# Feed-forward opening of a decoder layer: the LayerNorm chain of three tiles moved one step ahead, the first ten gate and up products put into two banks in turn, tile 0's butterflies moved between engines

## What is computed

```python
gate = bitlinear(x, w_gate)          # x: (4, 512, 512), w_gate, w_up: (2048, 512)
up = bitlinear(x, w_up)
intermediate = jax.nn.silu(gate) * up
return h_bitlinear(intermediate, w_down)     # w_down: (512, 2048)
...
def bitlinear(x, w):   return jnp.einsum('bsh,oh->bso', act_quant(x), weight_quant(w))
def h_bitlinear(x, w): return jnp.einsum('bsh,oh->bso', act_quant(fwht(x)), weight_quant(w))
```

## Time and profile before

| | us |
|---|---|
| median of 3 runs | 1610.19 |
| lowest and highest | 1608.81, 1610.94 |
| time of the profiled execution | 1610.17 |
| its span, first to last instruction | 1608.3 |
| PE busy in the span | 1542.3 (96%) |
| POOL busy | 1268.9 (79%) |
| DVE busy | 1235.6 (77%) |
| ACT busy | 1175.4 (73%) |
| feed-forward block in the span | from 1300.5 to the end |

### The profile page before, as it was taken

How to read it: one execution, slowest core, us unless ns; L and a number is a source line. 1 busy time by engine, 2 the same in 40 slices (tenths; PEclk the granted TensorE clock), 3 DMA queues, 4 the chain that set the end, 5 groups by cost and what they waited for, 6 DMA issues and landing times. The chain is left out here.

```text
span 1608.3 us, 23916 instructions
## 1 busy us (share of the span) xinstructions
PE 1542.3 (96%) x7487; PEld 1069.7 (67%) x7520; DVE 1235.6 (77%) x2254; ACT 1175.4 (73%) x1950; POOL 1268.9 (79%) x1141
## 2 busy tenths in 40 slices
PE   8989999999999998999999999999999978999997
PEld 4577787787788756666666666766656535666665
DVE  2499989878877756787977888778888676776776
ACT  2454556788755435999999899989998937887873
POOL 0487787787787724899999999999999949988870
PEclk9999999999999998999999999999999999999999
DMA  7324251433312005111312032101201230010000
GB/s 249 118 71 92 81 94 47 114 117 120 118 40 94 33 29 167 41 46 29 109 38 63 21 104 67 32 22 43 77 9 48 122 125 1 28 40 27 21 21 27
DMA packets 57190, 110.24 MB, mean 69 GB/s; under 512 B 9244, under 2 KB 13596, under 8 KB 56682
## 3 DMA queue, kind: packets, MB, share of 16 engines
q1 hardware_dynamic: 55488, 107.64, 22.4%
q10 hardware_dynamic: 1578, 1.07, 0.2%
HBM read 71.26 MB, written 18.88 MB: 56 GB/s over the span
## 5 line engine op out<-in xcount | busy, mean ns | idle before, releaser
L1443 POOL TENSOR_TENSOR x_p_lo<-x_p,x_p_hi 128x1024 fp32r<-128x1024 f32 x255 | 603.3, 2393 | 59.0 <-ACT x_p_hi L1209 34.5
L1345 DVE TENSOR_REDUCE x_maxes<-x_ps_a 128x1 f32<-128x1024 f32 x252 | 306.8, 1217 | 114.5 <-PE x_ps_a L1544 110.9
L1172 ACT ACTIVATE x_p<-x_ps_b,x_any_valid 128x1024 f32<-128x1024 f32 x256 | 285.0, 1113 | 55.5 <-PE x_ps_b L1524 49.6
L1209 ACT ACTIVATE x_p_hi<-x_p 128x1024 fp32r<-128x1024 f32 x256 | 271.2, 1059 | 6.3
L1524 PE MATMUL x_ps_b<-x_Q,x_K 103*128 103x512 f32 x512 | 218.9, 509 | 12.1 <-ACT x_p L1172 10.1
L1584 PE MATMUL x_ps_o<-x_p_hi,x_V 128*96 128x512 f32 x512 | 208.4, 407 | 2.8 <-POOL x_p_lo L1443 2.2
L1585 PE MATMUL x_ps_o<-x_p_lo,x_V 128*96 128x512 f32 x512 | 201.4, 393 | 0.0
L1544 PE MATMUL x_ps_a<-x_K,x_Q 99*128 99x512 f32 x504 | 164.5, 407 | 4.7 <-POOL x_Q L1431 2.8
L1524 PEld LDWEIGHTS x_ps_b<-x_Q,x_K 103*128 103x128 f32 x512 | 87.6, 191 | 106.2 <-issue 58.3
L447 ACT ACTIVATE a_aT_hi<-a_ps_a 128x512 fp32r<-128x512 f32 x64 | 38.3, 598 | 150.5 <-PE a_ps_a L732 124.1
L458 ACT ACTIVATE a_work<-a_ps_s,a_neg_max,a_q_r 128x128 f32<-128x128 f32 x256 | 114.1, 465 | 9.9 <-DVE a_neg_max L553 9.8
(11 more groups left out here) (297 smaller groups left out, 3992.0 us busy)
## 6 DMA issues: line engine op xcount, KB each, us to landing
shared<-in_L_ffn_w_gate SPq DMA_DIRECT2D x16, 512.0 KB, 4.0
shared<-in_L_ffn_w_up SPq DMA_DIRECT2D x16, 512.0 KB, 4.2
shared<-in_L_ffn_w_down SPq DMA_DIRECT2D x16, 512.0 KB, 4.2
shared<-in_ctx SPq DMA_DIRECT2D x8, 1024.0 KB, 7.4
x_scratch<-rows SPq DMA_DIRECT2D x31, 256.0 KB, 2.0
x_Q<-x_q_hi SPq DMA_DIRECT2D x112, 64.0 KB, 2.0
shared<-in_L_attn_out_w SPq DMA_DIRECT2D x6, 1024.0 KB, 8.3
ffn_quant<-shared SPq DMA_DIRECT2D x24, 256.0 KB, 4.5
```

Source lines behind the costliest of these rows:

```text
L1172: act.activation(p[:, v % 3, :, :], ps_b[:, :, :], ACT.Exp, scale=any_valid[:, b % 2:b % 2 + 1]).then_inc(exp_ready, 1)
L1209: act.activation(p_hi[:, r], p[:, v % 3], ACT.Copy).then_inc(hi_ready, 1)
L1345: dve.tensor_reduce(out=maxes[:, c % 2, 3 + r:4 + r], in_=scores_bank(n)[:, :, :], axis=mybir.AxisListType.XY, op=ALU.max).then_inc(max_re ...
L1443: pool.tensor_tensor(out=p_lo[:, v % 3, blocks], in0=p[:, v % 3, blocks], in1=p_hi[:, r, blocks].bitcast(F32), op=ALU.subtract)\
```

## The change

Four things change, all in `phase_feed_forward`.

1. `chain_step` replaces the fixed steps of the rows' chain. Tiles 1 and 2 (those below `SOONER = 3`; tile 0 has no chain here) have the steps of `stats`, `ln_rstd`, `ln_bias`, `h`, `h_max`, `hr` and `hq` one step sooner, the others where they were. The transposes into `ps_q` and `hqT` stay. The loop begins at step -2 to make room.
2. For steps below `FILL = 10` the gate product goes to `ps_t[c % 2]` and the up product to `ps_z[c % 2]`, and each waits for the silu or the `f` of two quarters before instead of one. From step 10 on they use `ps_g` and `ps_u` and wait as before. Where the banks come into their old use, waits are added.
3. Tile 0's second `between_quarters` goes from DVE to POOL, in step 4.
4. Tile 0's two `between_halves` stay on DVE, and go from step 5 to the ends of steps 7 and 8, behind the `f` of these steps.

```diff
+        FILL = 10
+        SOONER = 3
+
+        steps = range(-2, NQ + 22)
+
+        def chain_step(c, lag):
+
+            for shift in (0, 1):
+                m, i = divmod(c - lag + shift, 4)
+                if i == 0 and 1 <= m < TILES and (m < SOONER) == bool(shift):
+                    return m
+            return None
...
+        def gate_bank(c):
+            return ps_t[c % 2] if c < FILL else ps_g
+
+        def up_bank(c):
+            return ps_z[c % 2] if c < FILL else ps_u
...
-                if i == 1 and 1 <= n + 1 < TILES:
-                    m = n + 1
+                m = chain_step(c, -3)
+                if m is not None:
                     dve.wait_ge(rstd_ready, m)
                     dve.tensor_scalar(ln_bias[:, :], mv[:, 0:1], ln_rstd[:, :], -1.0, ALU.mult, ALU.mult).then_inc(ln_bias_ready, 1)
...
-                if i == 3 and n + 2 < TILES:
-                    m = n + 2
+                m = chain_step(c, -5)
+                if m is not None:
                     dve.wait_ge(x_in[m % XR], 16 * (m // XR + 1))
...
-                if i == 0 and quarter(c, 4) and n - 1 in VECTOR_TILES:
+                if i == 0 and quarter(c, 4) and n - 1 == TILES - 1:
                     between_quarters(dve, n - 1, 2)
-                if i == 1 and quarter(c, 5) and n - 1 in VECTOR_TILES:
+                if i == 1 and quarter(c, 5) and n - 1 == TILES - 1:
                     between_halves(dve, n - 1, 0)
                     between_halves(dve, n - 1, 1)
...
+                if c in (7, 8):
+                    between_halves(dve, 0, c - 7)
...
-                if i == 0 and quarter(c, 4) and n - 1 not in VECTOR_TILES:
+                if i == 0 and quarter(c, 4) and n - 1 < TILES - 1:
                     between_quarters(pool, n - 1, 2)
...
                 if quarter(c, 10):
                     m, j = quarter(c, 10)
                     pe.wait_ge(fB_ready, 2 * m + j // 2 + 1)
...
+                    if c < FILL + 2:
+                        pe.wait_ge(silu_ready, c - 1)
...
-                    if c >= 1:
+
+                    if c >= FILL:
                         pe.wait_ge(silu_ready, c)
+                    elif c >= 2:
+                        pe.wait_ge(silu_ready, c - 1)
...
-                    if c >= 1:
+                    if c >= FILL:
                         pe.wait_ge(f_ready, c)
+                    elif c >= 2:
+                        pe.wait_ge(f_ready, c - 1)
```

More of the change, by code:

```diff
@@ L1712, in phase_feed_forward @@
             sem(n) for n in ("z_round_ready", "zq_ready", "zqT_made", "zqT_ready", "down_ready", "out_ready"))
-        steps = range(-1, NQ + 22)
+        FILL = 10
[11 more added lines that the diff above has]
+            return ps_z[c % 2] if c < FILL else ps_u
         def quarter(c, lag):
             return divmod(c - lag, 4) if 0 <= c - lag < NQ else None
-        VECTOR_TILES = (0, TILES - 1)
         LAST = TILES - 4
@@ L1825, in _ @@
                         .then_inc(h_ready, 1)
-                if i == 2 and 1 <= n + 1 < TILES:
-                    m = n + 1
+                m = chain_step(c, -2)
+                if m is not None:
                     act.wait_ge(h_max_ready, 3 * m)
@@ L1964, in _ @@
                         dve.wait_ge(fC_ready, 4 * (n - 2) + 2 * (i // 2) + 2)
[L1965 removed]
+                    dve.tensor_tensor(out=f[:, n % 2, i * 512:(i + 1) * 512], in0=up_bank(c)[:, :], in1=gate[:, c % 2, :], op=ALU.mult)\
                         .then_inc(f_ready, 1)
+                if c in (7, 8):
+                    between_halves(dve, 0, c - 7)
         @block.gpsimd
@@ L1973, in _ @@
                 i, n = c % 4, c // 4
-                if i == 0 and 1 <= n + 1 < TILES:
-                    pool.wait_ge(var_ready, n + 1)
+                m = chain_step(c, -4)
+                if m is not None:
+                    pool.wait_ge(var_ready, m)
                     pool.tensor_tensor(out=ln_rstd[:, :], in0=ln_var[:, :], in1=half_neg[:, :], op=ALU.pow).then_inc(rstd_ready, 1)
-                if i == 0 and quarter(c, 4) and n - 1 not in VECTOR_TILES:
+                if i == 0 and quarter(c, 4) and n - 1 < TILES - 1:
                     between_quarters(pool, n - 1, 2)
-                if i == 1 and quarter(c, 5) and n - 1 not in VECTOR_TILES:
+                if i == 1 and quarter(c, 5) and 0 < n - 1 < TILES - 1:
                     between_halves(pool, n - 1, 0)
@@ L2012, in _ @@
                     cols = slice(i * 512, (i + 1) * 512)
-                    if c >= 1:
+                    if c >= FILL:
                         pe.wait_ge(silu_ready, c)
+                    elif c >= 2:
+                        pe.wait_ge(silu_ready, c - 1)
                     for k in range(DC):
-                        last = pe.matmul(ps_g[:, :], hqT[:, n % 2, k, :], wg[:, k, cols], start=(k == 0), stop=(k == DC - 1))
+                        last = pe.matmul(gate_bank(c)[:, :], hqT[:, n % 2, k, :], wg[:, k, cols], start=(k == 0), stop=(k == DC - 1))
                     last.then_inc(gate_ready, 1)
-                    if c >= 1:
+                    if c >= FILL:
                         pe.wait_ge(f_ready, c)
+                    elif c >= 2:
+                        pe.wait_ge(f_ready, c - 1)
                     for k in range(DC):
-                        last = pe.matmul(ps_u[:, :], hqT[:, n % 2, k, :], wu[:, k, cols], start=(k == 0), stop=(k == DC - 1))
+                        last = pe.matmul(up_bank(c)[:, :], hqT[:, n % 2, k, :], wu[:, k, cols], start=(k == 0), stop=(k == DC - 1))
                     last.then_inc(up_ready, 1)
@@ L2029, in _ @@
                         pe.wait_ge(zr_ready, k - 1)
+                    else:
+                        pe.wait_ge(f_ready, FILL)
                     for s in range(2):
```

3 lines of the change are left out of this document (1 added, 2 removed).

## The result

| | before | after |
|---|---|---|
| median, us | 1610.92 (1608.02 to 1613.19, 20 runs) | 1614.16 (1612.30 to 1616.65, 20 runs) |
| time of the profiled execution | 1610.17 | 1614.57 |
| its span | 1608.3 | 1612.7 |
| mean granted clock of PE in it | 0.994 | 0.990 |

The ratio of after to before is 1.0024, with a 95% interval of 1.0018 to 1.0030: **the change costs 3.24 us by the medians, and 2.9 to 4.8 us by this interval**. The forecast was 1610.5 us, with 1612.8 as its upper bound.

A forecast was written before the change was run, and what follows sets the result against it. POOL's gapless row was taken to set tile 4's transposes; an advance of up to 3.5 us, mostly eaten by POOL's hold, left them 0.3 us late: 1610.17 + 0.3 = 1610.5 us, range 1607.4 to 1612.8.

The forecast's parts named there:

- 0.3 us late: Tile 4's transposes, by which the sum goes, were to start at 1348.6 instead of 1348.34.
- S: Block's start: POOL's first `fC` at 1307.93, 0.27 us late, with tile 1's statistics ahead of `hqT`.
- DVE and ACT to the first `fB`: Opening, followed from S: `f` of step 7 at S + 11.95, the first `fB` 0.60 later at S + 12.55.
- It takes 1.14: Tile 0's first `fB` on DVE, behind step 7: 1.14 us, as two are 2.27 to the next start.
- The scales, the silu and `f` of step 8: Between tile 0's two `fB` on DVE: 1.38 us, putting the end of step 8's `f` at S + 15.07.
- Sum of the hold: POOL stands 3.8 us before tile 1's `fA`, until the second `fB` ends; tile 3's `ln_rstd` at 1327.3 instead of 1324.63.
- DVE is early for it now.: Tile 4: `h` follows `ln_rstd` by 0.27 us instead of 0.89, using up the 0.6 us of slack there.
- The low clock behind 4.4 us of idle: PE idle before step 10: later products issued low, free while no more than some 3 us of work run low.
- A microsecond won or lost before the full pipeline stays to the end, one for one, unless something later catches it.: From the opening to the kernel's end: what tile 4's transposes gain or lose, the kernel gains or loses.
- POOL isn't held: Faster rival at tile 1's `fA`: little or no hold, 1606.7 us in full, 1608.6 with half the hold gone; chance 0.15.
- the clock stays low: Slower rival, steps 10 to 13: 11.4 us of low clock cost 5.7, less 1.2, giving 1614.7 us; chance 0.11.
- The side that I gave 0.10: Slower by over 0.2%, above 1613.4 us; chance 0.10, most of the weight there the slower rival's.

The follow-up runs named there:

- fb_together: The changed kernel with both `fB` of tile 0 behind the `f` of step 7; 1611.6 us, ratio 1.0007 to the kernel before.
- fb_at_6: The changed kernel with both `fB` of tile 0 behind step 6 and tile 1's statistics behind tile 0's `hqT` again; 1611.55 us, ratio 1.0002 to before.
- pe_filled: The changed kernel with 20 unread matmuls in PE's 4.55 us idle before the up product of step 10; 1612.57 us, ratio 1.0015 to before.
- chain_only: The kernel before with only the chain of tiles 1 and 2 a step sooner; 1611.51 us, ratio 1.0002 to before.
- banks_only: The kernel before with only the two banks in turn for the first products; 1611.4 us, ratio 1.0002 to before.
- the fillings: Unread matmuls put into PE's idle stretches: in the opening in pe_filled (1612.57 us), in opening and drain in after_fill_both (1611.87 us).
- hqt_first: The changed kernel with tile 1's statistics behind tile 0's `hqT` again; 1615.5 us, ratio 1.0032 to before.
- after_fill_both: The changed kernel with 20 unread matmuls in the opening's idle and 9 and 15 in the drain's two idles; 1611.87 us, ratio 1.0004 to before.
- fb6_drain_fill: fb_at_6 with 9 and 15 unread matmuls in the drain's two idles; 1608.43 us, ratio 0.9988 to before.
- the two filled kernels: after_fill_both (1611.87 us), and the kernel before with 9 and 15 unread matmuls in the drain's two idles (1609.96 us).

## Why the prediction was wrong

It gave "0.3 us late" for tile 4's transposes, and nothing beyond. The profiles differ by 3.61 us from the block's start: 2.03 at tile 4's transposes, and 1.58 in the drain. By its steps, in time from the block's start:

- *The start.* S, POOL's first `fC`, was to be at rel. 7.37 (1307.93 less 1300.56); it was at 7.56. Right to 0.2: the clock rose 4.7 us behind the block's first transposes in both profiles, as assumed.
- *DVE and ACT to the first `fB`.* `f` of step 7 was to be at S + 11.95; it was at S + 11.92. Seven steps from rows of other places, right.
- *"It takes 1.14."* **This is the first term that was mis-sized.** The first `fB` held DVE 1.73 us (1321.44 to 1323.17). In the rows I took it from, at 1316.47, POOL stood; here it was in the middle of an `fC`, and DVE got going when that was all but done. The same instruction pair took 2.35 us before, 2.94 in fb_together, where it met one `fC`, and 3.42 in fb_at_6, where it met two, which were slowed as well. The Trainium skill ("SBUF — State Buffer", SBUF: two separate sides) says that a VectorE instruction with two inputs in SBUF and a GpSimd instruction that reads SBUF share a pair of ports by an exclusive lock: whichever starts first holds it to its end, and the other is blocked. The traces agree, with the turns of fb_at_6. Had I used it, the term would have been up to 1.27 us more for each `fC` met, an estimate from POOL's rows.
- *The scales, the silu and `f` of step 8*: 1.38 forecast, 1.72 measured. The silu began at once; the 0.34 lie between it and `f`, and no row says why.
- *Sum of the hold.* 3.8 forecast, 4.69 measured. Tile 3's `ln_rstd` was to be at rel. 26.74 and was at 27.94: 0.19 + 0.59 + 0.34, and 0.1 that no single step accounts for. From there to tile 4's 15.33, forecast 15.40. Tile 4's `ln_rstd` so came at rel. 43.27 instead of 42.1.
- *"DVE is early for it now."* Wrong. `ln_bias` of tile 4 started at 1345.87, 0.69 behind the end of `ln_rstd` (1344.62 + 0.56), so the slack was not used up. The products of tile 3 had run at the low clock, and the `fT_lo` ahead of `ln_bias` was late with them. In pe_filled, with the clock up, the transposes follow tile 4's `ln_rstd` by 5.89; here by 6.54. That is 0.65, and with the 1.1 that this `ln_rstd` was late it is the 1.8 between the forecast 48.0 and the measured 49.81.
- *The low clock behind 4.4 us of idle.* It was foreseen as a rival, of 11.4 us, and it came, with 10. Its price there was mis-sized the other way: 4.5 us forecast, 0.5 measured (pe_filled), since POOL's row and not PE set tile 4's time. Even so 1.06 us of idle were left ahead of tile 4's transposes; pe_filled had 2.03. The forecast's own "no more than some 3 us of work run low" was too short.
- *"A microsecond won or lost before the full pipeline stays to the end, one for one, unless something later catches it."* **This is the step that failed.** From tile 5 on the offset did stay at 2.03, tile after tile, up to tile 15. But in the last 40 us an idle of 2.3 us lay in wait, behind which the clock held in one profile and fell in the other: 1.38 of the further 1.58. The forecast had no term for the drain's idle stretches. They work against gains as much as against losses: chain_only and fb_at_6 were 1.3 and 1.7 us ahead of before at tile 5 and lost 1.4 and 1.7 there; banks_only lost 1.2 of 1.8.

What the clock does there is this case's own: the same 2.3 us of idle ahead of the same product, once at 1.00 behind it, once at 0.50. The Trainium skill ("TensorE: Matmul & The Clock Gate", What's actually happening) says that the clock follows how busy the array has been of late; the fillings bear that out, with 1.04 for 1.89 us in the opening and a window at 1.00 for 0.50 in the drain. When an idle of this length makes the clock fall, no run here shows. Behind the 2.0 us ahead of tile 4's transposes it fell in hqt_first and after_fill_both, and it held in pe_filled, fb_together, fb_at_6 and fb6_drain_fill. It isn't a matter of the kernel alone, for executions of one kernel differ. Over the changed kernel's 20 runs the mean granted clock goes with the time: four at 0.992 took 1612.3 to 1614.0 us, ten at 0.990 1613.4 to 1615.2, six at 0.987 or 0.988 1615.3 to 1616.7. Over 33 of the kernel before, nineteen at 0.994 took 1607.0 to 1611.9, seven at 0.990 1612.0 to 1613.5.

Of the rivals, "POOL isn't held" is refuted by the 4.69, and "the clock stays low" was right about the place and wrong about the price. The side that I gave 0.10 came: a sum of the mis-sized `fB`, the `f` that came late, the slack and a drain that no term covered. The opening's 2.03 alone gives 1612.2, the drain's 1.58 on top of the forecast 1612.1, both within the range. That 3.2 us could hardly be told from no change was too cautious: the interval of the ratio is 0.12% wide.

**What stays open.** How much of the 1.9 us between the two filled kernels is the hold, and how much the low clock behind tile 4, in most runs; why the `f` of step 8 came 0.34 late; and when a given idle lets the clock fall.
